# A 512-row fp32 projection turned into three products of fp32r halves

## What is computed

```python
x = x + tanh(g_xattn[0]) * first_attention(layernorm(x), ctx)       # both ways, with a gate
x = x + tanh(g_ffn[0])   * top2_of_8_experts(layernorm(x))
x = x + tanh(g_xattn[1]) * second_attention(layernorm(x), ctx)
x = x + tanh(g_ffn[1])   * mlp(layernorm(x))                        # ternary weights, 1024 wide

def second_attention(x, y):
    x_proj = relu(einsum('bxd,ed->bxe', x, W) + b)                  # the product that is changed
    y_proj = relu(einsum('byd,ed->bye', y, W) + b)
    att = softmax(einsum('bxd,byd->bxy', x_proj, y_proj))
    return einsum('bxy,byd->bxd', att, y)
```

## Time and profile before

| what | us |
|---|---|
| median of 3 runs | 1083.78 |
| lowest, highest | 1083.14, 1087.67 |
| the profiled execution | 1084.55 |
| its span, first to last instruction | 1082.6 |
| PE busy in it | 1026.4 |
| DVE busy | 506.4 |
| ACT busy | 479.9 |
| POOL busy | 305.6 |

### The profile page before, as it was taken

The page is one execution under the profiler, slowest core; times in us unless marked ns, Lnnn a source line. Parts: engine busy times, 40 slices in busy tenths (PEclk is TensorE's granted clock), DMA queues, the critical chain, the costliest instruction groups (busy, mean ns, idle before and its releaser), DMA issues.

```text
span 1082.6 us, 14392 instructions
## 1 busy us (share of the span) xinstructions
PE 1026.4 (95%) x5218; PEld 831.1 (77%) x5218; DVE 506.4 (47%) x1391; ACT 479.9 (44%) x877; POOL 305.6 (28%) x432
## 2 busy tenths in 40 slices
PE   7989998897999999999999999999999999999996
PEld 4757776665778987886789878867898788788885
DVE  6567766746633362555333624553336245133311
ACT  1345442643544453445444544454445345443431
POOL 0025553311161154222611442225114422012111
PEclk9989998998999999999999999999999999999999
DMA  9930001641266365342663744436637544344540
GB/s 333 375 104 2 2 3 57 220 153 40 83 213 225 137 214 156 117 136 88 224 228 117 228 147 125 125 94 234 210 129 222 156 121 152 117 128 145 152 139 22
DMA packets 44276, 158.93 MB, mean 147 GB/s; under 512 B 6448, under 2 KB 6832, under 8 KB 43306
## 3 DMA queue, kind: packets, MB, share of 16 engines
q0 software_dynamic: 29952, 104.88, 31.1%
q1 hardware_dynamic: 10826, 40.63, 10.9%
q10 hardware_dynamic: 3424, 12.45, 2.9%
HBM read 138.01 MB, written 29.36 MB: 155 GB/s over the span
## 4 chain that ended last, share of the span: by engine, by line
PE 75%; DVE 7%; POOL 6%; ACT 4%; issue 4%; DMA 3%; DVEq 0%; POOLq 0%; ACTq 0%
PE psum L987 48%; POOL slots L2227 4%; PE psum L870 2%; DMA slot_rows<-slots 2%; PE psum L893 2%; PE psum L1064 2%; PE psum L1066 2%; PE psum L1065 2%; PE psum L1040 1%; PE psum L692 1%; PE psum L668 1%; PE psum L706 1%; PE psum L880 1%; PE psum L722 1%; PE psum L605 1%
## 5 line engine op out<-in xcount | busy, mean ns | idle before, releaser
L2214 POOL DMA_DIRECT2D mlp_pieces<-in_mlp x176 | 96.9, 557 | 446.6 <-PE psum L987 440.2
L987 PE MATMUL psum<-hidden_a_high,mlp_pieces 128*128 128x512 f32 x512 | 208.0, 406 | 5.3 <-DVE hidden_a_low L2059 5.3
L987 PE MATMUL psum<-hidden_b_high,mlp_pieces 128*128 128x512 f32 x512 | 202.9, 396 | 0.0
L987 PE MATMUL psum<-hidden_a_low,mlp_pieces 128*128 128x512 f32 x512 | 201.5, 394 | 0.0
L987 PE MATMUL psum<-hidden_b_low,mlp_pieces 128*128 128x512 f32 x512 | 199.7, 390 | 0.0
L2059 DVE TENSOR_TENSOR hidden_a_low<-hidden_a,hidden_a_high 128x512 fp32r<-128x512 f32 x128 | 88.2, 689 | 177.3 <-ACT hidden_a_high L1455 176.7
L2059 DVE TENSOR_TENSOR hidden_b_low<-hidden_b,hidden_b_high 128x512 fp32r<-128x512 f32 x64 | 44.3, 693 | 175.0 <-ACT hidden_b_high L1455 148.2
L987 PEld LDWEIGHTS psum<-hidden_a_high,mlp_pieces 128*128 128x128 f32 x512 | 97.3, 190 | 29.8 <-DVE hidden_a_low L2059 7.6
L987 PEld LDWEIGHTS psum<-hidden_a_low,mlp_pieces 128*128 128x128 f32 x512 | 97.4, 190 | 22.0 <-issue 2.6
L1472 ACT ACTIVATE hidden_a<-psum,mlp_scales 128x512 f32<-128x512 f32 x64 | 44.2, 690 | 156.4 <-PE psum L987 156.3
L987 PEld LDWEIGHTS psum<-hidden_b_high,mlp_pieces 128*128 128x128 f32 x512 | 96.2, 188 | 20.1 <-issue 0.8
(11 more groups left out here) (290 smaller groups left out, 1832.0 us busy)
## 6 DMA issues: line engine op xcount, KB each, us to landing
mlp_pieces<-in_mlp POOLq DMA_DIRECT2D x176, 512.0 KB
slots<-in_zeros SPq DMA_DIRECT2D x3, 3072.0 KB, 37.5
yrows<-expert_rows ACTq DMA_DIRECT2D x18, 512.0 KB, 2.7
mlp_piece_to_examine<-in_mlp SPq DMA_DIRECT2D x16, 512.0 KB, 4.4
slot_rows<-slots SPq DMA_DIRECT2D x15, 512.0 KB, 4.9
x_residual<-in_x SPq DMA_DIRECT2D x4, 1024.0 KB, 24.3
out<-x_residual SPq DMA_DIRECT2D x8, 512.0 KB
expert_in<-in_Wi SPq DMA_DIRECT2D x1, 2048.0 KB, 16.0
```

The costliest lines, as they stand in the source:

```text
L987: last = mm(o, a, b, start=(k == 0 and i == 0), stop=(k == n_k - 1 and i == len(parts) - 1))
L2214: pool.dma_start(mlp_ring[:, r % RING, :], d["mlp"][r % NCHECK]).then_inc(ring_in[r % RING], 16)
```

## The change

The projection becomes three products of fp32r halves for each of its four fp32 ones: high weight by high x, low weight by high x, high weight by low x. For this

- ACT's copy writes fp32r (`xcT_h`) instead of fp32; its number and place stay.
- DVE gets `c_low(c)`: two subtractions (PSUM minus `xcT_h`), each behind one copy of ACT. In `b_last_pass` it stands behind `b_add` of m = 2; in the last stage at t = at, behind that column's `low` and ahead of `r_coef` and `r_rank`. PE waits for its semaphore `xTl_r`.
- DVE gets `halve_context_weight()` once, behind `b_add` of m = 1 of `b_last_pass`: cast, subtraction, copy over the loaded weight. PE waits for it at c = 0.
- To make room, the low x and the first cast share the space of `slot_rows_T_low`; six small tables of the routing lie over others that are dead by then, and three lie in another region.

```diff
+        w1l = place("weights", "context_weight_low", [P, KC, D], F32R)
...
+        xcT_l = place("weights", "x_norm_c_T_low", [P, KC, GN], F32R, at=cursor["weights"] - KC * GN * 4)
+        w1c = place("weights", "context_weight_high_made", [P, KC, D], F32R, at=cursor["weights"] - KC * GN * 4)
...
-        row4 = place("weights", "slot_row", [P, JT, 2])
-        eq = place("weights", "is_slot", [P, JT, E])
+        row4 = place("weights", "slot_row", [P, JT, 2], at=rtop_at)
+        eq = place("weights", "is_slot", [P, JT, E], at=rpex_at)
...
-        xcT = place("work", "x_norm_c_T", [P, KC, GN], at=xdl_at)
+        xcT_h = place("work", "x_norm_c_T_high", [P, KC, GN], F32R, at=xdl_at)
...
             def c_project(c):
-                pe.wait_ge(xTc_r, 2 * c + 2)
+                pe.wait_ge(xTl_r, 2 * c + 2)
+                if c == 0:
+                    pe.wait_ge(w1_r, 2)
                 for m in range(KC):
                     for k in range(KC):
-                        last = mm(ps[:, 2 + m, :], w1t[:, k, m * P:(m + 1) * P], xcT[:, k, :],
-                                  start=(k == 0), stop=(k == KC - 1))
+                        for i, (w, t) in enumerate(((w1h, xcT_h), (w1l, xcT_h), (w1h, xcT_l))):
+                            last = mm(ps[:, 2 + m, :], w[:, k, m * P:(m + 1) * P], t[:, k, :],
+                                      start=(k == 0 and i == 0), stop=(k == KC - 1 and i == 2))
                     last.then_inc(xp_ps, 1)
...
+            def c_low(c):
+                for pair in range(2):
+                    dve.wait_ge(xTc_r, 2 * c + pair + 1)
+                    t = slice(2 * pair * P, (2 * pair + 2) * P)
+                    dve.tensor_tensor(xcT_l[:, :, t], ps[:, pair, :].rearrange("p (k c) -> p k c", k=KC),
+                                      xcT_h[:, :, t].bitcast(F32), ALU.subtract).then_inc(xTl_r, 1)
+
+            def halve_context_weight():
+                st.link(dve.tensor_copy(w1c[:], w1t[:]))
+                dve.tensor_tensor(w1l[:], w1t[:], w1c[:].bitcast(F32), ALU.subtract).then_inc(w1_r, 1)
+                dve.wait_ge(w1_r, 1)
+                dve.tensor_copy(w1h[:], w1c[:].bitcast(F32)).then_inc(w1_r, 1)
+                dve.wait_ge(w1_r, 2)
...
                     b_add(g, s, m)
                     if m == 0:
                         c_norm(0)
+                    if m == 1:
+                        halve_context_weight()
+                    if m == 2:
+                        c_low(0)
...
                             low(c, full, part, rest, 3 * HC * n + HC * (layer + 1) + c + 1)
                             t = HC * layer + c
+                            if b is not None and t == at:
+                                c_low(n + 1)
                             if s is not None and t == 0:
                                 r_coef(s)
                             if s is not None and t == 1:
```

More of the change, by code:

```diff
@@ L186, in program @@
         cf = place("weights", "batch_weight", [P, JT, E])
+        rk_at = cursor["weights"]
         rk = place("weights", "rank", [P, JT + 1, E])
@@ L191, in program @@
         vi = place("weights", "slot_number_integer", [P, JT, 2], I32)
-        qi = place("weights", "slot_tile_and_chunk", [P, 2, JT, 2], I32)
-        qf = place("weights", "slot_tile_and_chunk_value", [P, 2, JT, 2])
-        row4 = place("weights", "slot_row", [P, JT, 2])
-        eq = place("weights", "is_slot", [P, JT, E])
+        kept = cursor["weights"]
+        qi = place("weights", "slot_tile_and_chunk", [P, 2, JT, 2], I32, at=rk_at)
+        cursor["weights"] = kept
+        kept = cursor["weights"]
+        qf = place("weights", "slot_tile_and_chunk_value", [P, 2, JT, 2], at=rk_at + 2 * JT * 2 * 4)
+        cursor["weights"] = kept
+        kept = cursor["weights"]
+        row4 = place("weights", "slot_row", [P, JT, 2], at=rtop_at)
+        cursor["weights"] = kept
+        kept = cursor["weights"]
+        eq = place("weights", "is_slot", [P, JT, E], at=rpex_at)
+        cursor["weights"] = kept
         ti = place("weights", "count_integer", [P, E], I32)
@@ L202, in program @@
         sbase = place("weights", "slot_base", [P, E])
-        e24 = place("weights", "tile_past_expert", [1, EB, E])
-        esum = place("weights", "tile_experts_past", [1, EB])
-        iota = place("weights", "tile_numbers", [1, EB])
-        eid = place("weights", "tile_expert_column", [1, NSB, EB], I32)
+        kept = cursor["weights"]
+        e24 = place("weights", "tile_past_expert", [1, EB, E], at=rmarked_at)
+        cursor["weights"] = kept
+        esum = place("small", "tile_experts_past", [1, EB])
+        iota = place("small", "tile_numbers", [1, EB])
+        eid = place("small", "tile_expert_column", [1, NSB, EB], I32)
         tri = place("weights", "triangle", [P, P])
@@ L291, in program @@
         EC = place("work", "probs_c", [P, G, L])
+        w1t_at = cursor["work"]
         w1t = place("work", "context_weight", [P, KC, D])
+        w1h = place("work", "context_weight_high", [P, KC, D], F32R, at=w1t_at)
         ypT = place("work", "context_projected_T", [P, KC, BL])
```

10 lines of the change are left out of this document (8 added, 2 removed).

## The result

The changed kernel took 1089.18 us (median of 17 runs, 1084.29 to 1092.85), the kernel before 1084.83 us (17 runs in between, 1081.00 to 1087.73). The ratio is 1.0037, interval 1.0021 to 1.0053: **4.0 us slower** (2.3 to 5.7), where the forecast was 4.6. A second series, with other runs of both, gave 1.0023 (1.0010 to 1.0035), 2.5 us slower. So "no change by more than 0.5%" held, and both times lay within the range, 1089.18 us 0.8 above the forecast of 1088.4. Whether the terms of the sum were right is another question. Two of them were, one was too large, and one stood for something that the runs don't show. One run of a later experiment (delay_twice), 1161.85 us at a mean clock of 0.839, belongs to a slower state and is left out of its ratio.

A forecast was written before the change was run, and what follows sets the result against it. PE, busy 95% of the span, was taken as the bound. +0.7 (last expert pass), +3.6 (groups 0, 2, 4), -2.9 (groups 1, 3, 5, 6), +3.2 (clock) gave +4.6 on 1083.78: 1088.4 us, range 1081.5 to 1092.0.

The forecast's parts named there:

- Check (a): Projection on PE: 96 records at a pace of 0.227 us, 2.7 us each time.
- The first place: Last expert pass, group 0 of the second attention: halving free, 1.45 us of new PE wait, net +0.7 us.
- check (b): Near 224, before the first projection: a PE wait of 1.3 to 1.8 us, released by DVE.
- The routed groups: Last stage's groups 0, 2, 4, which route tokens: subtractions delay slots, PE's wait grows 0.3 to 2.2 us; +3.6 us.
- (c): On DVE: the rank copy comes 1.2 us further behind the hidden_b subtraction before it.
- (d): PE's waits for slot_rows of about 2.2 us, three times; staying at 0.3 us would make the prediction wrong.
- (f): No PE wait before the projection in the seven places other than the last expert pass.
- Check (e): A window of granted clock below 1 behind two of PE's three waits for slot_rows.
- Rival 1: The clock doesn't fall at the new waits, everything else as forecast: +1.4 us, 1085.2 us; chance 0.20.
- Rival 2: Routed groups: DMA traffic, not scatter start, sets slot arrival; -2.2 us (1081.6), or -4.4 (1079.4); chance 0.12 for both.
- rival 3: The clock falls at all four new waits, last expert pass included: +7.8 us, 1091.6 us; chance 0.15.
- Rival 4: Low-weight fp32r products run slower, or fp32 ones overlapped more; savings shrink towards 0: +8.3 us, 1092.1; chance 0.03.

The follow-up runs named there:

- delay_twice: The changed kernel with two unused DVE reductions of 512 columns added ahead of the rank chain in the three routed groups: 1092.81 us, ratio 1.0073 to the kernel before.
- after_again: The changed kernel run once more, nothing altered, in a second series: 1087.02 us, ratio 1.0023 to the kernel before.
- before_subtractions: The kernel before, fp32 product kept, with the two DVE subtractions added in groups 0 to 6, their result unused: 1088.05 us, ratio 1.0030 to the kernel before.
- products_rank_early: The changed kernel without low-half subtractions (third product uses high x) and with DVE's rank chain moved to t = 0: 1075.90 us, ratio 0.9926 to the kernel before.
- rank_early: The changed kernel with DVE's rank chain moved from t = 1 to t = 0, ahead of the subtractions: 1081.10 us, ratio 0.9966 to the kernel before.

## Why the prediction came out near, and which steps didn't hold

**The saving** was sized at 0.72 us a place and is 0.63, 5.1 us for eight instead of 5.8. The step that failed is the transfer of 0.227 us from the products of the MLP to the new ones. These step by 0.233, twelve times. The nearest row had the right pace: the products of the expert pass, in the kernel before, ten steps in 2.32 us, 0.232 each:

```profile
221.65 0.39 PE L870 MATMUL psum<-expert_low,x_T_high 128*128 128x512 f32 x1
...
223.97 0.40 PE L870 MATMUL psum<-expert_high,x_T_low 128*128 128x512 f32 x1
```

Check (a) holds in count and not in pace. The gain of 0.86 that the Trainium skill's four passes ("FP8 and Floating Point Precision", "TensorE Precision Notes") would give was further off.

**The first place** held nearly. The delay from start to start, as the prediction counted it, is 1.33 us instead of 1.45; the 1.17 of the list lies below the 1.3 to 1.8 of check (b). The halving was free, and the wait at the end of the pass is unchanged at 4.2 us. By the stretch of the pass the net is 33.70 - 32.94 = +0.8, up to the last stage +0.6 (66.04 in after_again, 65.49 before), predicted +0.7.

**The routed groups** held in mechanism and in size. The rank copy moved by 1.20 us (c). The six waits of the two profiles have a mean of 2.2 us, the number that was predicted (d), though single ones go from 1.5 to 3.0, and no wait stands before the other seven projections (f). Late slots cost PE 7.4 - 1.5 = 5.9 us more than before in the three groups, and the sum had 5.8 (3 x 1.9).

**The clock** is the term that failed. The step was to extend the fall behind one wait of 1.78 us to waits of 2.2 us: +3.2 us for two falls in three routed groups. Check (e) finds none in either profile. The changed kernel's mean clock over 29 runs is 0.979, and 0.9785 over 75 runs of before: no lower, where two more falls would make it 0.003 lower. In the profiles of all kernels, waits for slots of 1.25 to 2.97 us were followed by a fall in 1 of 12 cases, those of 3.04 us and more in 4 of 4. The wait for `hidden_a_low` of 1.77 us, which every kernel has three times, was followed by one in 11 of 36. In before's profile it was 2 of 3 (one of them is in the earlier trace rows), a high draw, and to extend it to a longer wait was a guess from one case.

**The sum as it is now:** -5.1 (products), +1.4 (first place), +5.9 (slots), 0 (clock) = +2.2 us. The profiles agree: the last stage, counted from its first wait for `hidden_a_low`, takes 799.67 us before with two falls and 799.57 in both profiles of the changed kernel with one, so +1.5 at equal falls, and the way to it adds +0.6 to +0.8. Brought to the clock of before with 0.86 us for 0.001, the slope of its own line, the two profiled executions stand at +2.3 and +2.9 us. The second series gave 2.5, the first 4.0, and all runs together are 4.2 apart at equal clock. So 1 to 2 us of the loss are in runs that have no trace and stand in no term; their cause is open.

Rival 1, no fall, is the mechanism that the profiles show, with terms that gave 0.8 us too little. That the forecast's 4.6 lay near the 4.0 was luck: 3.2 us for falls that don't occur stood in the place of 0.8 us in the other terms and of a rest that no term explains. Rival 2 is excluded by delay_twice and before_subtractions, rival 3 by the clock's mean and the windows. Rival 4 is excluded by products_rank_early.

## What to carry to other kernels

A faster product pays only where PE's next input isn't late already, so look for the waits of a few tenths behind the edit: they show a path without slack, and a delay upstream lands there nearly whole (1.1 to 1.5 us for 1.4 in delay_twice). Work that is added on a side engine belongs into a gap that two others leave, ahead of its reader and not ahead of the longest chain. Their order was worth about as much as the product: rank_early gained 6 to 8 us over the changed kernel, some 2 of which the kernel before gains by the same move, against 5.1 for the product. So compare a change with the kernel before that has the same repair. A fall of the clock in one profile is one draw: count such waits over several traces, and compare the mean clock of many runs, before it becomes a term of a sum. And count waits from start to start, since the idle time of a list begins at the end of a record.

## What was not expected of the hardware

- Three products of fp32r halves take 2.80 us where four fp32 products took 3.44, 0.81 of them and not three quarters.
- A cast of 128x512 from fp32 to fp32r on DVE took 0.46 and 0.43 us, a subtraction of the same size 0.69.
- A scatter (an indirect DMA that POOL issues) takes 0.96 to 1.0 us, but up to 1.49 when it starts just behind the start of a 0.69 us subtraction of 128x512 from SBUF on DVE: 35 of 35 long ones in twelve traces. Such a step delays everything behind it on this path.
- After a wait the first fp32r product of 512 columns is followed by the next only after 0.34 us (225.20 to 225.54) instead of 0.23.
